# Stacked halves of z for the mixing of q and k, and the weight split on GpSimd, in a two-stage attention and feed-forward kernel

## The reference

```python
# layer 1: a 64x64 matrix for each sample mixes its tokens, then one head of attention with width 256
h   = einsum('bct,bcd->bdt', x, cond_weights[itok])
qkv = h @ Wqkv + bqkv
x   = x + softmax(q @ k^T / 16) @ v @ Wo + bo
# layer 2: a 1024x1024 matrix for each sample, chosen by itok, then a linear layer with a routed low-rank term
y   = einsum('bsi,boi->bso', x, cond2_weight[itok])
x   = x + y @ W^T + b + routed_lora(y)
```

## Time and profile before

| | |
|---|---|
| median of 3 runs (lowest, highest) | 2286.02 us (2283.11, 2287.87) |
| time of the profiled execution | 2283.59 us |
| its span, first to last instruction | 2281.9 us |
| busy: TensorE, DVE, ACT, POOL | 2246.7, 1236.8, 953.2, 61.3 us |
| DMA: moved, mean rate | 356.46 MB, 156 GB/s |
| granted TensorE clock | 0.999 |

### The profile page before, as it was taken

How to read it: one execution, slowest core, us unless ns; L and a number is a source line. 1 busy time by engine, 2 the same in 40 slices (tenths; PEclk the granted TensorE clock), 3 DMA queues, 4 the chain that set the end, 5 groups by cost and what they waited for, 6 DMA issues and landing times.

```text
span 2281.9 us, 73807 instructions
## 1 busy us (share of the span) xinstructions
PE 2246.7 (98%) x28506; PEld 1748.9 (77%) x28506; DVE 1236.8 (54%) x3438; ACT 953.2 (42%) x2461; POOL 61.3 (3%) x128
## 2 busy tenths in 40 slices
PE   7999999999999889999999999999999999999998
PEld 4777777777777678887878787878787878787876
DVE  7777777777777754343434444444344444434443
ACT  5776767677767643232322222222222222222221
POOL 4000000000000000000000000000000000000000
PEclk9999999999999999999999999999999999999999
DMA  7668777777677743141214141214225132231303
GB/s 290 249 255 303 272 269 284 272 264 280 245 283 276 271 180 113 44 144 38 93 58 149 39 158 66 76 38 151 74 69 193 39 112 84 103 112 39 131 20 112
DMA packets 108960, 356.46 MB, mean 156 GB/s; under 512 B 27600, under 2 KB 28752, under 8 KB 79184
## 3 DMA queue, kind: packets, MB, share of 16 engines
q1 hardware_dynamic: 98640, 280.89, 34.1%
q0 software_dynamic: 10112, 72.36, 8.5%
HBM read 218.99 MB, written 134.22 MB: 155 GB/s over the span
## 4 chain that ended last, share of the span: by engine, by line
PE 96%; DVE 2%; DMA 1%; ACT 1%; issue 1%; POOL 0%; SPq 0%; DVEq 0%; ACTq 0%; POOLq 0%; PEldq 0%
PE bank L1179 21%; PE bank L1315 19%; PE bank L1284 19%; PE bank L1286 10%; PE bank L1317 10%; PE bank L1136 4%; PE bank L1138 4%; PE bank L1137 4%; PE bank L1297 1%; PE bank L1324 1%; PE bank L1325 1%; PE bank L1299 1%; DMA w<-ws 0%; DVE wf L875 0%; PE bank L1231 0%
## 5 line engine op out<-in xcount | busy, mean ns | idle before, releaser
L1284 PE MATMUL bank<-xs,w 128*128 128x128 f16 x8192 | 625.1, 219 | 3.9 <-DVE xs L882 2.0
L1179 PE MATMUL bank<-w,xs 128*128 128x384 f16 x3072 | 553.2, 327 | 4.4 <-DVE w L895 4.4
L1315 PE MATMUL bank<-y,wf 128*128 128x512 f16 x2048 | 483.8, 379 | 0.8 <-DVE xr L925 0.8
L1284 PEld LDWEIGHTS bank<-xs,w 128*128 128x128 f16 x8192 | 478.2, 98 | 5.8 <-issue 2.4
L763 ACT ACTIVATE zh<-bank 128x256 f32<-128x256 f32 x256 | 97.8, 382 | 777.1 <-PE bank L1286 774.1
L1179 PEld LDWEIGHTS bank<-w,xs 128*128 128x128 f16 x3072 | 290.6, 98 | 165.0 <-issue 2.8
L1286 PE MATMUL bank<-xs,w 128*128 128x64 f16 x8192 | 405.8, 193 | 0.0
L921 DVE SCALAR_TENSOR_TENSOR xr<-bank,xr 128x256 f32 (+1 forms) x256 | 108.6, 424 | 432.7 <-PE bank L1325 387.5
L1315 PEld LDWEIGHTS bank<-y,wf 128*128 128x128 f16 x2048 | 196.9, 98 | 186.6 <-DVE xr L925 1.1
L1286 PEld LDWEIGHTS bank<-xs,w 128*128 128x128 f16 x8192 | 335.9, 98 | 0.0
L1317 PE MATMUL bank<-y,wf 128*128 128x256 f16 x2048 | 265.4, 273 | 0.0
(11 more groups left out here) (158 smaller groups left out, 2083.9 us busy)
## 6 DMA issues: line engine op xcount, KB each, us to landing
stage<-w_in SPq DMA_DIRECT2D x68, 1024.0 KB, 8.8
w<-ws POOLq DMA_DIRECT2D x68, 1024.0 KB, 6.1
ws<-wf SPq DMA_DIRECT2D x64, 1024.0 KB, 6.9
out<-xr SPq DMA_DIRECT2D x128, 256.0 KB, 2.3
xr<-x_in SPq DMA_DIRECT2D x31, 1024.0 KB, 8.0
x<-xr SPq DMA_DIRECT2D x31, 1024.0 KB, 4.4
xr<-x SPq DMA_DIRECT2D x124, 256.0 KB, 3.5
wcf<-wc_in SPq DMA_DIRECT2D x128, 32.0 KB, 4.5
```

The source lines that it names most:

```text
L1179: e = mm(zps[q % 2][h][:, 0:384], lhs, rhs[:, k, h * 384:(h + 1) * 384], start=(k == 0 and lhs is a and rhs is wq_h), stop=(k == K - 1 and ...
L1284: mm(both, hi[:, k, c], x_k, start=(k == 0), stop=False)
L1315: mm(fps[m % 2][:, :], wf_h[:, k, c], yhl[:, u, k, :], start=(k == 0), stop=False)
```

## The change

1. z's halves for q and k are stacked on the partitions: for sample b of the pair, `zs[:, r, b, :]` holds the high half in one set of 64 partitions and the low half in the other. The matrix of the sample is loaded twice into `wcf`, one under the other (a second DMA), so one matmul of 128 rows computes (high + low) by the matrix. TensorE's mixing is 16 matmuls of 64 columns. z is split 512 + 256 over its two banks; k's products go to a z bank of the pair (`kps`), q's stay in `qps`; v's halves have tensors of their own (`zvh`, `zvl`).
2. ACT and DVE no longer split weight units. POOL loads, splits and stores all of them, in its own loop behind the sorting, by two tensor_scalar and one tensor_tensor for each half of a unit. The four units of W follow, then the loads of the first condition and of the first samples. These were paced through stage A before.
3. At the start SP issues the second half of the first group of x later and no unit; two small weight chunks are split in the first round of stage A instead of at the start of stage B; TensorE's wait for the output weights stands at the first output product.
4. At the end the last group's output is stored in three parts (`TAIL`).

```diff
+TAIL = ((0, 4), (4, 6), (6, 8))
...
+        ZCOLS = ((0, 2 * DH), (2 * DH, 3 * DH))
+        qps, kps, chps, wops = bank[4], [bank[0], bank[2]], bank[5], [bank[6], bank[7]]
...
+        def qk_block(r, c):
+            return qps[:, c * P:(c + 1) * P] if c < 2 else kps[r][:, (c - 2) * P:(c - 1) * P]
...
@@ SP @@
+                    again = wcf[(1 - b) * S:(2 - b) * S, n, b * S:(b + 1) * S]
+                    sp.dma_start(again, wc_in[bass.ds(e, 1), :, 0, :].rearrange("a c d -> (a c) d")
+                                 ).then_inc(s_wc[n], 16)
...
-                    unit_turn(*here, load=not late_units)
...
-                    unit_turn(here[0], here[1] + 1, load=not late_units)
...
@@ GpSimd @@
-                    if n == 0:
-                        pool.wait_ge(s_z, PACE * (t + 1))
-                    else:
+                    if n > 0:
...
+            def load_unit(i, q):
...
+                pool.dma_start(stage[:, q % 2, :], src).then_inc(s_unit[q % 2], 16)
+            def split_unit(i, q, final=False):
+                high, low = unit_halves(q, q if final else None)
+                wait(pool, s_unit[q % 2], i, 32, 16 * (q // 2) + 16)
...
+                halves = [slice(n, n + T) for n in range(0, UNIT, T)]
+                for c in halves:
+                    st = stage[:, q % 2, c]
+                    pool.tensor_scalar(high[:, c], st, SW, 1.0, ALU.mult, ALU.mult).then_inc(s_uhi, 1)
+                    pool.tensor_scalar(st, st, SW, 1.0, ALU.mult, ALU.mult).then_inc(s_uhi, 1)
+                for h, c in enumerate(halves):
+                    wait(pool, s_uhi, i, 16, 4 * q + 2 * h + 2)
+                    pool.tensor_tensor(low[:, c], stage[:, q % 2, c], high[:, c], ALU.subtract).then_inc(s_ulo, 1)
+            def units(i, last=False):
+                for q in range(4):
+                    split_unit(i, q)
+                    wait(pool, s_ulo, i, 8, 2 * q + 2)
+                    dst = ws[bass.ds(i, 1), :, q, :, :].rearrange("a p h n -> (a p) h n")
+                    pool.dma_start(dst, split_w[:, q % 2, :, :]).then_inc(s_us[q % 2], 16)
+                    load_unit(i if q < 2 else i + 1, (q + 2) % 4)
...
+            for q in range(4):
+                split_unit(NC, q, final=True)
...
             load_condition(0)
             first_slots()
...
@@ ScalarE @@
+                for b in range(2):
+                    at = slice(b * S, (b + 1) * S)
+                    nc.scalar.activation(zs[at, q % 2, b, :], zps[q % 2][0][at, :], Copy,
+                                         scale=SZ / (SX * SW)).then_inc(s_zh, 1)
+                nc.scalar.activation(zvh[:, q % 2, :], zps[q % 2][1][:, 0:DH], Copy,
+                                     scale=SZ / (SX * SW)).then_inc(s_zh, 1)
...
-                    unit_hi(i, q, (0, 1))
...
@@ VectorE @@
+                for b in range(2):
+                    wait(dve, s_zh, i, 12, 3 * q + b + 1)
+                    at, other = slice(b * S, (b + 1) * S), slice((1 - b) * S, (2 - b) * S)
+                    v.scalar_tensor_tensor(out=zs[other, q % 2, b, :], in0=zps[q % 2][0][at, :],
+                                           scalar=SZ / (SX * SW), in1=zs[at, q % 2, b, :], op0=ALU.mult,
+                                           op1=ALU.subtract).then_inc(s_zl, 1)
...
                 for c in range(4):
-                    e = v.scalar_tensor_tensor(out=qkl[:, c, :], in0=qkps[:, c * P:(c + 1) * P],
+                    wait(dve, s_qkh, i, 8, 2 * q + c // 2 + 1)
+                    e = v.scalar_tensor_tensor(out=qkl[:, c, :], in0=qk_block(q % 2, c),
...
-                    unit_lo(i, q, (2,))
...
@@ TensorE @@
-                for c in range(4):
-                    d = slice(c * P, (c + 1) * P)
-                    e = three(qkps[:, d], [(zh[:, r, d], zl[:, r, d], wch[:, r, 0:P], wcl[:, r, 0:P])])
+                for b in range(2):
+                    at = slice(b * S, (b + 1) * S)
+                    for c in range(4):
+                        dst, z_c = qk_block(r, c)[:, at], zs[:, r, b, c * P:(c + 1) * P]
+                        mm(dst, z_c, wch[:, r, at], start=True, stop=False)
+                        e = mm(dst, z_c, wcl[:, r, at], start=False, stop=True)
```

More of the change, by code:

```diff
@@ L484, in _ @@
             body_b(IB - 1, last=True)
-            store_out(IB - 1, 1)
-            for u in range(2):
-                sp.wait_ge(s_out[u], 64 * IB)
+            rs = batches(IB - 1, 1)
+            for lo, hi in TAIL:
+                sp.wait_ge(s_res, FA + 16 * IB - K + hi)
+                for b, r in enumerate(rs):
+                    sp.dma_start(out[bass.ds(r, 1), :, lo * S:hi * S].rearrange("a p n -> (a p) n"),
+                                 group_cols(GB - 1, b * BT + lo * S, (hi - lo) * S)).then_inc(s_out[1], 16)
+            sp.wait_ge(s_out[0], 64 * IB)
+            sp.wait_ge(s_out[1], 64 * (IB - 1 + len(TAIL)))
         @block.gpsimd
@@ new lines, in split_unit @@
+            def split_unit(i, q, final=False):
+                high, low = unit_halves(q, q if final else None)
+                wait(pool, s_unit[q % 2], i, 32, 16 * (q // 2) + 16)
+                pool.sem_inc(s_turn_pool, 1)
+                if final and q == 0:
+                    for n in range(2):
+                        pool.wait_ge(s_us[n], 32 * IA)
+                        pool.sem_inc(s_turn_pool, 1)
+                    pool.wait_ge(s_wl, NCH)
+                    pool.sem_inc(s_turn_pool, 1)
+                elif not final:
+                    wait(pool, s_us[q % 2], i, 32, 16 * (q // 2))
+                    pool.sem_inc(s_turn_pool, 1)
+                halves = [slice(n, n + T) for n in range(0, UNIT, T)]
[6 more added lines that the diff above has]
+                    pool.tensor_tensor(low[:, c], stage[:, q % 2, c], high[:, c], ALU.subtract).then_inc(s_ulo, 1)
@@ L624, in _ @@
+            units(0)
+            with pool.Fori(1, NC - 1) as i:
+                units(i)
+            units(NC - 1, last=True)
+            for q in range(4):
+                split_unit(NC, q, final=True)
+                if q < 2:
+                    wait(pool, s_ulo, NC, 8, 2 * q + 2)
+                    load_unit(NC, q + 2)
             load_condition(0)
@@ L656, in _ @@
                 chunk_hi(n)
[L657 to L671, removed]
+            mix_hi(0, 0)
+            x_hi(0, 1)
             def out_chunks(i, u, ms, phase_b=False):
@@ L867, in _ @@
             assert done[0] == S_SLOT
[L869 to L874, removed]
-                    v.scalar_tensor_tensor(out=low[:, lo:hi], in0=stage[:, q % 2, lo:hi], scalar=SW,
-                                           in1=high[:, lo:hi], op0=ALU.mult, op1=ALU.subtract).then_inc(s_wul, 1)
             def x_lo(i, q, b, phase_b=False):
@@ L904, in _ @@
                     link(dve_copy(2, UPTO, trps[0:NC, 0:1]))
-                if n == 5:
-                    mix_lo(0, 0)
-                if n == 6:
-                    for b in range(2):
-                        x_lo(0, 1, b)
+            mix_lo(0, 0)
+            for b in range(2):
+                x_lo(0, 1, b)
             def residual(i, u, ms, phase_b=False):
@@ L957, in a_step @@
                 e.then_inc(s_qkl, 1)
-                if end:
-                    unit_lo(i, q, (0,))
-                else:
+                if not end:
                     mix_lo(i, q + 1)
@@ L1100, in b_step @@
                         x_lo(i, q + 1, b, phase_b=True)
-                if first and q == 0:
-                    chunk_lo(K + 4)
-                    chunk_lo(K + 5)
                 y_set(i, q, 2)
                 y_set(i, q, 3)
-                if first and q < 2:
-                    for n in range(2 * q, 2 * q + 2):
-                        unit_lo(IA, n, range(NPC), n)
                 if before:
@@ L1171, in z_part @@
                     wait(pe, s_xl, i, 4, q + 1)
-                    wait(pe, s_zl, i, 4, q - 1)
+                    wait(pe, s_zl, i, 12, 3 * (q - 1))
                 for k in ks:
```

131 lines of the change are left out of this document (40 added, 91 removed).

## The result

The changed kernel takes 2554.26 us (median of 4 runs, 2552.25 to 2555.75) against 2285.11 us for the kernel before on the same chip (4 runs): a ratio of 1.118, 95% interval 1.116 to 1.120. The forecast was 2273 us and its range ended at 2318. The sign is wrong and so is the size.

The account below looks back on a forecast made before the run. TensorE, without gaps in stage A, was taken as the bound. Gains 12.2 + 3.7 + 3 + 0.5 less 6.4 made 13.0 us off 2283.6: 2270.6, or 2273 us on the runs' footing; range 2260 to 2318.

Parts of the forecast that it names:

- DVE behind POOL: Stage A: DVE instructions waiting for a POOL instruction that came first; allowed 0.1 us a pair, 6.4 us lost.
- Mixing, 12.2 us: TensorE, stage A: 16 matmuls of 64 columns replace 12 of 128; 0.19 us gained a pair, 12.2 us over 64.
- Halves of z, at nothing: TensorE's z split 512 + 256: as many columns at the same cost per column, so no gain or loss.
- Start, 3.7 us: First pairs: TensorE's waits for the output weights (2.3 us) and ptl (1.4 us) go; 3.7 us gained.
- POOL's unit, 10.4 us: POOL's loop in stage A: loading, splitting and storing one weight unit takes 10.4 us, 68 units ending at 752.
- the 13% for POOL standing still: POOL's loop: share of time POOL stands still while DVE reads two SBUF inputs, 13% of an 11.9 us pair.
- The point of decision at 10.66: POOL's time per unit above which it decides the kernel's time; each 0.1 us above costs 6.8 us.
- POOL is late: Rival, between the stages: units take 11.8 us, stage B begins 77 us behind; middle 2310 us, 2273 to 2350; chance 0.28.
- Passage and end, 3.5 us: Between stages, shorter waits for condition weights and DVE's routing chain, 3 us; at the end, a smaller last part, 0.5 us.
- SyncE's mixing DMAs, at nothing: Stage A: the second mixing DMA goes out a pair or more ahead, so it costs nothing.
- TensorE waits for DVE behind POOL: Rival, stage A: x_lo delayed by a running POOL instruction; 0.4 us a pair, 26 us lost, 2293 us; chance 0.18.

Follow-up runs that it names:

- the run with pauses: Changed kernel with POOL waiting on its own semaphore behind each of six split instructions: 2463.52 us; the 80.2 us gap is from its version with mixing matrices first, 2346.89 us.
- the run with pauses and the matrices first: Changed kernel with POOL pausing behind each of six split instructions, and SyncE issuing mixing matrices ahead of its wait for the x1 store: 2346.89 us, ratio 1.027.
- faster loop, runs of 3.2 us: Changed kernel with fewer POOL pauses, store and next load inside the next unit, first condition ahead of W, mixing matrices first: 2303.02 us, ratio 1.008.

## Why the prediction was wrong

**The step that failed** is the term "DVE behind POOL": "I allow 0.1 us a pair, 6.4 us lost". It measured 207.9 us of waiting, and some 75 us of slower matmuls behind the gaps. Three things in it were wrong.

1. *The wrong instructions.* It looked at x_lo and wcl, which have two SBUF inputs, and overlooked pn, whose inputs and output all lie in SBUF and for which TensorE waits next. The runs show pn, x_lo and wcl held, whichever comes first; the reciprocal was not, and why it differs was not tested.
2. *The length of a hold.* The rival took the rest of one POOL instruction, 2.15 us at most. The hold lasts to the end of what POOL runs without a pause: 8.2 us for a unit, up to 15.6 for two; the runs with pauses show that it ends there.
3. *The evidence.* "In the rows DVE does not" wait was read from the earlier trace rows, where POOL's small instructions wait for one another's semaphores. Each is a run of its own; those rows could not show what six in a row do. The prediction says itself that no row shows DVE blocked, and still puts the term at 0.1 us.

The Trainium skill, SBUF — State Buffer, section "SBUF: two separate sides", which stood beside the rival, names two kinds of DVE instruction, those in a 2-port perf mode and those with two SBUF inputs, and says that whichever side starts first has the shared ports for the whole instruction. The rows agree for x_lo and wcl, which have two inputs, and on the release when there is a pause. Whether pn runs in such a mode no row shows by itself (0.29 us from SBUF, 0.35 from PSUM). The section speaks of one instruction; of a hold over several queued ones (7.68 us over six) it gives no price.

**The other terms.**

- *Mixing, 12.2 us:* right. In the changed kernel behind 780 us, where POOL is idle, the sixteen matmuls take 0.46 us (0.48 forecast), and a pair 11.83 us, 0.21 less than the earlier trace rows, as the same row of the pair before shows at 812.79:

```profile
812.79 0.49 PE L1149 MATMUL bank<-w,xs 128*128 128x512 f16 x2
...
824.16 0.19 PE L1191 MATMUL bank<-wch,zs 128*128 128x64 f16 x1
...
824.62 0.49 PE L1149 MATMUL bank<-w,xs 128*128 128x512 f16 x2
```

- *Halves of z, at nothing:* right where the pieces of units are gone or moved (11.83 and 11.85 us a pair). With the pieces in their old places, the first part of the change alone is 27.5 us slower.
- *Start, 3.7 us:* the transpose of the third pair starts at 52.01 and not at 55.20, 3.2 us earlier, 0.4 of them from two mixings.
- *POOL's unit, 10.4 us:* 10.11 (first instructions at 429.01 and 439.12). The two-input price was right (2.13 for 2.15 us), the one-input one low (1.01 from start to start, not 0.87), and the 13% for POOL standing still much too high: DVE was the one that stood. So the sum came near by luck: some 1.0 us too little for the instructions, the wait and the issues, and 1.4 too much for standing still. The point of decision at 10.66 was sound. At 11.8 us the rival *POOL is late* priced a 77 us gap, and the run with pauses measured 80.2.
- *Passage and end, 3.5 us:* from the start of stage B to the end 7.2 us were gained (1474.7 us against 1481.9), the routing chain's 2.8 us among them. POOL was done 320 us before, not 18 as forecast, so this says little of the passage that was meant.
- *SyncE's mixing DMAs, at nothing* ("a pair or more ahead"): true of the changed kernel, where ACT waits 5.1 us for them in all. In the run with pauses it waits 152.6 us, since SyncE stands at the store of x1 first.

The rival *TensorE waits for DVE behind POOL* named the mechanism, with ptl and ul as the places, but at 0.4 us a pair; the price was some 8 (20.2 us for 11.83).

## What to carry to other kernels

Before moving elementwise work to GpSimd, list every VectorE instruction whose tensors all lie in SBUF (here all but a 128x1 reciprocal were held) and who waits for it; price each at the whole run of GpSimd instructions without a pause, not at one. If GpSimd must work beside such a chain, put a semaphore wait between its instructions and read from PSUM what can be read there, then count the pauses in GpSimd's own time. Look for evidence against a contention only in rows where both sides are as long and as dense as they will be.

## What the runs showed of the hardware

- VectorE and GpSimd: an SBUF-only VectorE instruction of 128x128 or more, one input (7.68 us) or two (7.41, 7.43), waited through six GpSimd instructions on end, 1.04 to 2.1 us each, and once through twelve (15.60); a pause of 0.18 us between two of them let it in. DVE instructions that also read a PSUM bank were not held, nor was a 128x1 reciprocal in SBUF (0.16 us). The same tensor_scalar from PSUM took 0.35 us beside them.
- VectorE and GpSimd ran in step. Pairs took 20.2 us, two turns of POOL's loop. In the run with pauses and the matrices first, POOL's first ten turns took 11.3 to 11.8 us and the next 45 averaged 11.83, the time of a pair. That the hold does this is likely, but no run tests it by itself.
- TensorE's granted clock was 0.83 and 0.84 in stretches with a gap of 5.3 to 6.8 us in each pair, and 1.00 in those without. It was also 1.00 where gaps were at most 1.4 us (faster loop, runs of 3.2 us).
